# State-space stage: the sums that GpSimd adds up are accumulated by TensorE in two PSUM banks, and the decay factors go through a ring of two banks

## The reference

```
xm, z = split(x @ W_in.T, 2);  xc = silu(causal_conv4(xm) + conv_b)
dt, Bm, Cm = split(xc @ W_xproj.T, [64, 80])
delta = softplus(dt @ W_dt.T + b_dt);  A = -exp(A_log)
h_t[e,n] = exp(delta_t[e] * A[e,n]) * h_(t-1)[e,n] + delta_t[e] * Bm_t[n] * xc_t[e]
y_t[e] = sum over n of h_t[e,n] * Cm_t[n]  + D_skip[e] * xc_t[e]
out = (y * silu(z)) @ W_out.T
```

## Time and profile before

| | |
|---|---|
| time, median of 3 runs | 2523.08 us (2521.75 to 2523.22) |
| the profiled execution's own time | 2524.58 us |
| its span, first to last instruction | 2522.9 us |
| TensorE busy | 1929.5 us (76%) |
| VectorE busy | 1720.8 us (68%) |
| ScalarE busy | 1149.4 us (46%) |
| GpSimd busy | 1451.6 us (58%) |
| mean granted TensorE clock | 0.848 |

### The profile page before, as it was taken

One profiled execution on the slowest core, in us unless ns is written; L12 is line 12 of the kernel. 1 busy time (PEld: TensorE's weight loads), 2 busy tenths in 40 slices (PEclk: granted clock), 3 DMA queues, 4 the chain that ended last, 5 costly groups with the idle time before them and its releaser, 6 DMA issues. The chain is left out here.

```text
span 2522.9 us, 35893 instructions
## 1 busy us (share of the span) xinstructions
PE 1929.5 (76%) x10268; PEld 1489.8 (59%) x10269; DVE 1720.8 (68%) x3375; ACT 1149.4 (46%) x1897; POOL 1451.6 (58%) x1018
## 2 busy tenths in 40 slices
PE   6786969697878778697399999911979686599980
PEld 2455545464545454555299999911756475599970
DVE  1788888888888888886744444456963897644438
ACT  2676767767686767674232232312521442111112
POOL 1789899989989898986133333322211530255542
PEclk9887979697978878797599999965988897699995
DMA  2101111111101010100511111142000012222216
GB/s 69 38 30 48 33 48 34 47 34 36 47 26 51 31 52 30 50 33 24 221 41 46 50 46 48 44 138 85 1 17 11 1 34 108 91 71 71 66 59 197
DMA packets 77370, 139.12 MB, mean 55 GB/s; under 512 B 10449, under 2 KB 48465, under 8 KB 76450
## 3 DMA queue, kind: packets, MB, share of 16 engines
q1 hardware_dynamic: 63586, 100.19, 11.9%
q0 software_dynamic: 13632, 37.24, 4.7%
HBM read 105.38 MB, written 32.01 MB: 54 GB/s over the span
## 5 line engine op out<-in xcount | busy, mean ns | idle before, releaser
L778 DVE TENSOR_TENSOR_SCAN a_hs<-a_dA,a_carry,a_hs 128x512 f32<-128x512 f32 x512 | 637.0, 1268 | 28.1 <-POOL a_hs L400 24.2
L400 POOL TENSOR_TENSOR a_hs<-a_u,a_b_bc 128x1024 f32<-128x1024 f32 x258 | 625.4, 2427 | 0.4
L924 PE MATMUL a_h_ps<-k_ident,a_hs 128*128 128x128 f32 x2064 | 339.8, 317 | 186.1 <-DVE a_hs L778 114.3
L924 PEld LDWEIGHTS a_h_ps<-k_ident,a_hs 128*128 128x128 f32 x2064 | 284.0, 164 | 305.1 <-DVE a_hs L778 137.1
L554 ACT ACTIVATE a_dA<-a_delta,a_a_neg 128x512 f32<-128x512 f32 x512 | 351.5, 688 | 109.3 <-DVE a_hs L778 107.1
L412 POOL TENSOR_TENSOR a_acc<-a_acc,a_part 128x512 f32<-128x512 f32 x242 | 324.5, 1342 | 72.9 <-ACT a_part L568 71.3
L743 DVE SCALAR_TENSOR_TENSOR a_acc<-a_h_ps,a_c_tok,a_acc 128x512 f32<-128x512 f32 x242 | 177.2, 732 | 116.1 <-PE a_h_ps L924 116.1
L568 ACT ACTIVATE a_part<-a_h_ps,a_c_tok 128x512 f32<-128x512 f32 x242 | 165.6, 684 | 148.0 <-PE a_h_ps L924 134.4
L1224 POOL DMA_INDIRECT expert_rows<-m0e_ys,k_pair x71 | 74.1, 1043 | 236.4 <-DVE m0e_ys L1280 225.2
L1290 DVE TENSOR_TENSOR m0e_hT<-m0e_gs,m0e_u 128x512 f32<-128x512 f32 x70 | 48.1, 687 | 186.8 <-ACT m0e_gs L1243 186.8
L1243 ACT ACTIVATE m0e_gs<-m0e_g 128x512 f32<-128x512 f32 x71 | 42.4, 597 | 269.7 <-PE m0e_u L1321 269.7
(11 more groups left out here) (431 smaller groups left out, 3756.5 us busy)
## 6 DMA issues: line engine op xcount, KB each, us to landing
a_b_bc<-b_rows SPq DMA_DIRECT2D x132, 256.0 KB, 3.1
q_y<-expert_rows SPq DMA_DIRECT2D x32, 512.0 KB, 5.6
a_xl<-in_L_attn_x SPq DMA_DIRECT2D x9, 512.0 KB, 3.5
norm_rows<-a_shared SPq DMA_DIRECT2D x9, 512.0 KB, 2.9
m0w_up<-in_m_up SPq DMA_DIRECT2D x1, 4096.0 KB, 12.2
m0w_gate<-in_m_gate SPq DMA_DIRECT2D x1, 4096.0 KB, 21.8
m0w_down<-in_m_down SPq DMA_DIRECT2D x1, 4096.0 KB, 32.2
q_xl<-in_L_attn_x SPq DMA_DIRECT2D x8, 512.0 KB, 3.4
```

The costliest lines, as they stand in the source:

```text
L400: pool.tensor_tensor(hs[n % NBUF][:, half, :], u[s][:, half, :], b_bc[:, n % NBUF:n % NBUF + 1, :].broadcast_to([P, 2, T]), ALU.mult).then ...
L778: dve.tensor_tensor_scan(hs[k][:, c, :], dA[c][:], hs[k][:, c, :], carry[:, hf, c, n:n + 1], ALU.mult, ALU.add).then_inc(s_scan, 1)
L924: last = pe.transpose(hT_ps[j % 2][:, c * P:(c + 1) * P], hs[(n - 1) % NBUF][:, c, j * P:(j + 1) * P], ident[:])
```

## The change

Two of the four banks of `dA` become `sum_ps`, in which TensorE accumulates what GpSimd added. `weighted` now always writes `part`, and a new `pile` multiplies it by the identity into its bank, over all 16 states of a unit (a matmul that starts the bank in state 1 and one that closes it in state 0 of the next unit). ScalarE's `copy_sums` brings the two banks to `acc` in state 1, ahead of y0. The decay factors use the two banks that are left in turn, so that a factor waits for the scan two places back, and ScalarE's order shifts by two factors: `factor(n, 2)`, `weighted(n, 1)`, (in state 1 the copies,) `factor(n, 3)`, the carry, `MID_ACT`, `factor(n+1, 0)`, `weighted(n, 3)`, `factor(n+1, 1)`, `END_ACT`. The end of the stage takes its four output banks from both kinds.

```diff
+        RING = 2
+        dA = [m.ps(f"dA{c}", [P, T]) for c in range(RING)]
+        sum_ps = [m.ps(f"sum{k}", [P, ED]) for k in range(EC - RING)]
+        last_y = dA + sum_ps
...
-            pool.sem_inc(s_add, NO)
+            pool.memset(part[:], 0.0).then_inc(s_prep, 1)
...
-            def add(U, n, j, s):
-                if j not in OFF or n == 1:
-                    return
-                pool.wait_ge(s_part, part_count(U, n, j))
...
-                pool.tensor_tensor(acc[s][:, j, :], acc[s][:, j, :], part[:, j // 2, :], ALU.add).then_inc(s_add, 1)
...
                         for q in range(2):
                             product(U, n + 1, q, hf if n + 1 < NS else 1 - hf)
-                            add(U, n, 2 * q + 1, hf if n else 1 - hf)
...
             def factor(U, n, c, s):
                 k = n % NS
-                act.wait_ge(s_scan, lin(U, NS * EC, (n - 1) * EC + c + 1 + SCANNED))
-                act.activation(dA[c][:], delta[s][:, c, :], ACT.Exp, scale=a_neg[:, c, k:k + 1]).then_inc(s_da, 1)
+                act.wait_ge(s_scan, lin(U, NS * EC, last_scan(n, c) + 1 + SCANNED))
+                act.activation(dA[slot(n, c)][:], delta[s][:, c, :], ACT.Exp, scale=a_neg[:, c, k:k + 1]).then_inc(s_da, 1)
+
+            def copy_sums(U, s):
+                for k, j in enumerate(PILED):
+                    act.wait_ge(s_sum, piled(U, 0, j))
+                    act.activation(acc[s][:, j, :], sum_ps[k][:], ACT.Copy).then_inc(s_sumc, 1)
...
-                if n == 1:
+                if n == 1 and j == OFF[0]:
                     act.wait_ge(s_free[side("ct")], count("ct", before(U)))
-                    to = acc[s][:, j, :]
-                else:
-                    act.wait_ge(s_add, added_count(U, 0, j) + -NO if n == 0 else added_count(U, n - 1, j))
-                    to = part[:, j // 2, :]
+                act.wait_ge(s_sum, piled(U, n - 1, j))
+                to = part[:, j // 2, :]
...
+                        factor(U, n, 2, hf)
                         weighted(U, n, 1, here)
-                        factor(U, n + 1, 0, there)
+                        if n == 1:
+                            copy_sums(U, 1 - hf)
+                        factor(U, n, 3, hf)
...
-                        factor(U, n + 1, 1, there)
+                        factor(U, n + 1, 0, there)
                         weighted(U, n, 3, here)
...
-                        factor(U, n + 1, 2, there)
+                        factor(U, n + 1, 1, there)
...
                         for name in END_ACT.get(n, []):
                             task(name)
-                        factor(U, n + 1, 3, there)
...
                     if whole == "y0":
                         pe.wait_ge(s_acc, lin(U, NS * ND, 2 * ND))
-                        pe.wait_ge(s_add, lin(U, ADDS, 2 * NO))
+                        pe.wait_ge(s_sumc, lin(U, NPL, NPL))
...
+            def pile(U, n, j):
+                pe.wait_ge(s_part, part_count(U, n, j))
+                if n == 1:
+                    pe.wait_ge(s_sumc, lin(U, NPL, PILED.index(j) + 1))
+                pe.matmul(sum_ps[PILED.index(j)][:], ident[:], part[:, j // 2, :], start=n == 1, stop=n == 0).then_inc(s_sum, 1)
...
+            for k in range(NPL):
+                pe.matmul(sum_ps[k][:], ident[:], z[1][:, 0, :], start=True, stop=False)
...
                         turn(U, n, 0)
                         turn(U, n, 1)
+                        if n != 1:
+                            pile(U, n - 1, 3)
                         for name in EARLY.get(n, []):
                             task(name, U, F, 1 - hf)
                         turn(U, n, 2)
                         turn(U, n, 3)
+                        pile(U, n, 1)
+                        if n == 0:
+                            pile(U, 0, 3)
                         for name in LATE.get(n, []):
                             task(name, U, F, 1 - hf)
```

More of the change, by code:

```diff
@@ L184, in mamba_phase @@
         taps = hs[1]
-        dA = [m.ps(f"dA{c}", [P, T]) for c in range(EC)]
+        RING = 2
+        dA = [m.ps(f"dA{c}", [P, T]) for c in range(RING)]
+        sum_ps = [m.ps(f"sum{k}", [P, ED]) for k in range(EC - RING)]
+        last_y = dA + sum_ps
         hT_ps = [m.ps(f"h_ps{k}", [P, ED]) for k in range(2)]
@@ L226, in mamba_phase @@
         s_part = m.sem("weighted_by_act")
-        s_add = m.sem("summed_by_pool")
+        s_sum = m.sem("summed_by_pe")
+        s_sumc = m.sem("sum_copied")
         s_carry = m.sem("carry")
@@ L258, in mamba_phase @@
         ON = tuple(j for j in range(TJ) if j not in OFF)
-        ND, NO, ADDS = len(ON), len(OFF), len(OFF) * (NS - 1)
+        ND, NO, PILED = len(ON), len(OFF), OFF
+        NPL = len(PILED)
         def count(name, U):
@@ L286, in part_count, with slot, last_scan, piled @@
             return lin(U, NS * NO, NO * n + OFF.index(j) + 1 + NO)
-        def added_count(U, n, j):
-            return lin(U, ADDS, NO * (n - 1 if n > 1 else 0) + OFF.index(j) + 1 + NO)
+        SLOT = [g % RING for g in range(NS * EC)]
+        if RING == 3:
+            SLOT[-1] = 1
+        def slot(n, c):
+            return SLOT[(n * EC + c) % (NS * EC)]
+        def last_scan(n, c):
+            g = n * EC + c - 1
+            while SLOT[g % (NS * EC)] != slot(n, c):
+                g -= 1
+            return g
+        def piled(U, n, j):
+            return lin(U, NS * NPL, NPL * (n + 1) + PILED.index(j) + 1)
         ROWS = R + 2 * NS
         N_WEIGHTS = 16 * 11
-        N_PREP = 1 + EC + 8
+        N_PREP = 1 + EC + 9
         PER_D = 2 * (2 + 2)
@@ L446, in _ @@
             end = (0, 2 * NB, None)
-            for j in OFF:
-                add(end, 0, j, 1)
             rms(TILES - TJ, lambda per_: per_ * (2 * NB + 1))
@@ L587, in _ @@
                     softplus_ln(F0, 0)
-                    for c in range(EC):
+                    for c in range(RING):
                         act.wait_ge(s_delta, c // 2 + 1)
-                        act.activation(dA[c][:], delta[0][:, c, :], ACT.Exp, scale=a_neg[:, c, 0:1]).then_inc(s_da, 1)
+                        act.activation(dA[slot(0, c)][:], delta[0][:, c, :], ACT.Exp, scale=a_neg[:, c, 0:1]).then_inc(s_da, 1)
                 evac(name, None, F0, 0, silu=True)
@@ L651, in _ @@
                 weighted(end, 0, j, 1)
+            copy_sums(end, 1)
             act.wait_ge(s_free["Y"], len(FSEQ["Y"]) + 2 * NB * len(SEQ["Y"]) + 2)
@@ L777, in scan @@
                             dve.wait_ge(s_da, lin(U, NS * EC, n * EC + c + 1))
-                            dve.tensor_tensor_scan(hs[k][:, c, :], dA[c][:], hs[k][:, c, :],
+                            dve.tensor_tensor_scan(hs[k][:, c, :], dA[slot(n, c)][:], hs[k][:, c, :],
                                                    carry[:, hf, c, n:n + 1], ALU.mult, ALU.add).then_inc(s_scan, 1)
@@ L823, in _ @@
                 dve.wait_ge(s_yl, c + 1)
-                dve.tensor_tensor(z[1][:, c, :], dA[c][:], z[1][:, c, :], ALU.mult).then_inc(s_yg, 1)
+                dve.tensor_tensor(z[1][:, c, :], last_y[c][:], z[1][:, c, :], ALU.mult).then_inc(s_yg, 1)
             t_end = TILES - TJ
@@ L932, in _ @@
             pe.wait_ge(s_prep, N_PREP)
+            for k in range(NPL):
+                pe.matmul(sum_ps[k][:], ident[:], z[1][:, 0, :], start=True, stop=False)
+            pe.sem_inc(s_sum, 1)
             with pe.Fori(0, NB) as i:
@@ L948, in _ @@
                 turn(end, 0, j)
+                if j == 1:
+                    pile(end, -1, 3)
+            for j in PILED:
+                pile(end, 0, j)
             pe.wait_ge(s_acc, lin(end, NS * ND, 2 * ND))
-            pe.wait_ge(s_add, lin(end, ADDS, 2 * NO))
-            pe.wait_ge(s_da, 2 * NB * NS * EC + EC)
+            pe.wait_ge(s_sumc, (2 * NB + 1) * NPL)
+            pe.wait_ge(s_da, 2 * NB * NS * EC + RING)
             for c in range(EC):
-                output(dA[c], c, 1).then_inc(s_yl, 1)
+                output(last_y[c], c, 1).then_inc(s_yl, 1)
             pe.wait_ge(s_yg, EC)
```

## The result

Beside each other on one chip: before 2522.67 us median (2521.75 to 2523.22), after 2586.48 us (2582.34 to 2589.40), ratio 1.0252, 95% interval 1.0234 to 1.0270. The profiled execution of after took 2586.99 us, its span is 2585.3. 2586 lies inside the stated range of 2532 to 2602, but above the forecast's own, 2540 to 2580.

The account below looks back on a forecast made before the run. TensorE bounds states 4 to 8, GpSimd only 14 and 15, ScalarE and VectorE the long tasks between. Terms sum to +4.5 us a unit, +36 over 8 units, +2 once: 2561 us, range 2532 to 2602 (own 2540 to 2580).

Parts of the forecast that it names:

- Clock lost at the seam: Rival: states 14 to 0 at half clock until TensorE catches up, +5 instead of +1.5 a unit, 2589; chance 0.17.
- New matmuls, +8.6: States 4 to 8: ten new TensorE matmuls at 0.86 us in a stretch without a gap, +8.6 us a unit.
- the matmuls hide: Rival: states 4 to 8 absorb the new matmuls, each under 0.56 us; -5.6 us a unit, 2478; chance 0.08.
- Two banks, state 3, +1.3 later: State 3: halo tasks stand behind scan 1, so the convolution starts late and state 4's transposes come 1.3 us later.
- State 9, +0.1: State 9: SiLU holds ScalarE both before and after, so only the new matmuls around it show, +0.1 us a unit.
- Softplus, -4.0: States 10 to 13: VectorE's fix, subtract and add run faster beside an idle GpSimd; state 14 begins 4.0 us earlier.
- The rival in which contention stays: Rival: VectorE's contention stays or ScalarE's tasks stall the ring more, -0.5 instead of -4.0 a unit, 2589; chance 0.12.
- States 14 and 15, -3.0: States 14 and 15: without adds GpSimd no longer bounds them, VectorE does; 15.2 becomes 12.2 us, -3.0 a unit.
- Clock, +1.5: Unit's seam, states 14, 15 and 0: added matmuls where TensorE runs near half clock, taken as +1.5 us a unit.
- the prediction's bound of +5: Upper end of the 0 to +5 us a unit that the clock at the seam could cost.
- Once, +2: Outside the units: two clearing matmuls and two fewer factors ahead in the front, about +2 us once.

Follow-up runs that it names:

- halo_early: The changed kernel with ScalarE's halo tasks of state 3 moved ahead of factor (3, 3); 2578.19 us, ratio 1.0207.
- before_fill: The kernel before with two matmuls of zero weights per unit ahead of y0; 2508.93 us, ratio 0.9939.
- late_halo: The changed kernel with halo tasks early, GpSimd adding states 1 to 10, TensorE 11 to 15 and 0, merged in state 12; 2535.87 us, ratio 1.0038.
- fill: The changed kernel with ten zero-weight matmuls a unit on TensorE, before y0 and in states 0, 9 and 13; 2557.72 us, ratio 1.0123.
- ring_only: The kernel before with only the decay factors in two banks and ScalarE's order shifted, GpSimd still adding; 2576.41 us, ratio 1.0205.
- ring_halo: ring_only with state 3's halo tasks moved ahead of factor(3, 3); 2558.89 us, ratio 1.0132.

## Why the prediction was right, and where its sum fell short

The sign and the range held; 2586 is 25 us above the 2561 of the forecast, outside the forecast's own 2540 to 2580, and within 3 of the rival "Clock lost at the seam" (2589, chance 0.17). By the prediction's own steps:

- **New matmuls, +8.6**: right. 44.84 us against 44.85 forecast, 0.87 us each; the rival "the matmuls hide" (under 0.56) is out.
- **Two banks, state 3, +1.3 later**: right in the full change, 9.25 us (9.2 forecast), and halo_early takes 1.35 of it away again. **State 9, +0.1**: the mean is +0.2, but by luck. It is 9.49 us in the units at full clock and 11.18 in the others. At full clock the kernel with four banks takes 8.60 (before_fill, every second unit), so the change costs 0.9 here, and in half of the units a higher clock than the 0.83 of before gave it back. With the ring alone it is 11.90. That the ring is nearly free was wrong as a statement on the ring; it was right only for the ring under this longer stretch and with GpSimd idle.
- **Softplus, -4.0**: right, 36.29 (36.0 forecast); fix, subtract and add at 2.34. The rival in which contention stays is out. late_halo shows the other side: with GpSimd's products beside it the fix takes 5.52 us.
- **States 14 and 15, -3.0**: counted from 15.21 us, in a window that ends 0.7 us behind the next unit's first scan (763.70, not 764.40); from the mean of 14.92 it is -2.7. The mechanism is right, the size came only with full clock and no loop turn: 14.77 us after, 12.97 with the loop written out, 12.22 with fillers in units without a turn.
- **Clock, +1.5**: this is the term that was mis-sized. A unit of fill without a loop turn ahead of it or in it would be 27.7 + 9.25 + 44.84 + 9.49 + 35.95 + 12.22 = 139.45 us; the forecast's path without its clock term is 139.55. That they agree so closely is luck in part: states 0 to 2 are 0.5 longer than forecast and state 9 is 0.6 shorter. Everything that the real unit has above that, 145.10 - 139.45 = 5.65 us, is clock and loop turn. The fillers give back 3.4 of it, the written-out loop 1.4. With the loop written out a unit is 143.37 us, so the clock's own share is 3.9: nearer to the prediction's bound of +5 than to its +1.5. An argument against the rival was misread: the clock does not hold in states 1 to 8 of the kernel before, it is 0.75 over states 0 to 2 and 0.50 until y0 starts.
- **The rival came near by luck too.** It has TensorE at half clock from state 14 to state 0. In fact the new matmuls raised the granted clock there, to between 0.81 and 1.00 in states 14 and 15 (0.56 to 0.57 before) and 0.88 to 0.95 in states 0 to 2 (0.74 to 0.86 before). The time came near its 2589 because half clock in part of these states cost more than +1.5, and because the loop turn, which it doesn't have, adds 1.4 us a unit. The Trainium skill ("TensorE: Matmul & The Clock Gate", PE-mode transpose) says that transposes do not warm the clock; that the seam, mostly transposes, was slow before, and that matmuls, the new ones and those of zero weights, raise it, agrees, but no run here put transposes in the fillers' place, so that rule itself stays untested.
- **Loop turn**: a step that the prediction doesn't have. Its share is 7.3 us of the 64, 1.4 us a unit in the profiles.
- **Once, +2**: the first scan starts 1.9 us earlier (78.97 against 80.90), not 2 later, so 4 us less.

Sum: 4.05 us a unit above forecast (145.10 - 141.05) times 8 is 32, less 4 is 28; measured 25. Behind state 14 of the last unit the profile of the changed kernel is 4.8 us shorter than that of the kernel before. What stays open is why states 9 and 14 to 2 take different lengths in different units of one execution (141.6 to 148.9 us a unit). With the loop written out the units agree from the second on (143.35 to 143.40 us), which points to the turn and the clock, but what sets it in a given unit was not found.

## What to carry to other kernels

An engine that is the busiest on average (GpSimd here, 125 of 136.6 us) can be the bound in one short stage only. Move its work only for the stages in which it sets the pace, and leave it where the engine that would take it over has no gap: the same adds moved for all states cost 2.5%, and moved for eight of sixteen, with the lulls of TensorE mended, gained 1.5%. Two fillers a unit in the kernel before give 0.6% alone; what all the repairs would give there was not measured, so the adds' own share of the 1.5% is open. A buffer taken from a ring has to be priced at each long task on the engine that fills it, by a run with the ring alone, since other parts of the change can hide it.

## What was not expected of the hardware

- A wait on TensorE can cost a second time, behind it, and the same wait need not. Behind 2.39 us eight convolution instructions took 5.01 to 5.15 us in five units of ring_only and 3.54 in three; behind 0.81, 1.04 and 1.53 us (before, ring_halo, after) they took 3.54 in all. Behind its wait of 1.9 us in the changed kernel the first quarter of y0 took 1.85 us in three units and 2.26 to 3.48 in five.
- Idle work can pay: with two matmuls of zero weights ahead of y0 in each unit the kernel before is 16 us faster.
- The back edge of a loop: VectorE and TensorE stood 3.75 and 4.83 us with nothing pending. The kernel before has the same loop and gains nothing when it is written out; VectorE waits there anyway, 1.13 us for a factor.
- Two VectorE instructions of 128x1024 with two SBUF operands: 2.33 us beside an idle GpSimd, 5.52 beside one that multiplies; GpSimd's own pair of products took 5.65 us there and 4.66 to 4.69 in states where VectorE ran its scans.
- A matmul cut from 512 to 4 columns is not free: 0.14 us from start to start, and 0.1 more on the instruction behind it, against 0.87.
